# Row scores of the first attention layer's first two heads, taken from the whole K and a masked query instead of the stacks

## The reference

```python
q = proj(query, w_q, b_q)            # (2, 16, 256, 8), query = layernorm(x)
k = proj(key, w_k, b_k)              # (2, 16, 512, 8), key = value = ctx_1024
v = proj(value, w_v, b_v)
scores = einsum('bhqd,bhkd->bhqk', q, k) / sqrt(8)
scores = where(mask == 0, -1e9, scores)
attn = softmax(scores, axis=-1)
x = einsum('bhqk,bhkd->bhqd', attn, v)
```

## Time and profile before

| | us |
|---|---|
| median of 3 runs | 253.52 (252.95 to 254.31) |
| the profiled execution | 252.5 |
| its span, first to last instruction | 250.7 |

### The profile page before, as it was taken

How to read it: one execution, slowest core, us unless ns; L and a number is a source line. 1 busy time by engine, 2 the same in 40 slices (tenths; PEclk the granted TensorE clock), 3 DMA queues, 4 the chain that set the end, 5 groups by cost and what they waited for, 6 DMA issues and landing times.

```text
span 250.7 us, 5109 instructions
## 1 busy us (share of the span) xinstructions
PE 222.7 (89%) x1656; PEld 138.6 (55%) x1656; DVE 185.8 (74%) x578; ACT 156.1 (62%) x228; POOL 79.5 (32%) x228
## 2 busy tenths in 40 slices
PE   2879889999999999989897889999988989989970
PEld 1464445555555558976785444444534447768760
DVE  7779776777777476678558988888775657789974
ACT  6775897677875761521323567877767674796660
POOL 4581445465612100100201252444412042344321
PEclk9999999999999999999999999999999999999999
DMA  6779899921010048600050773300000000000000
GB/s 210 271 220 162 198 164 173 327 67 43 24 65 0 3 90 167 124 0 0 9 165 18 276 230 95 97 3 0 4 0 3 0 1 3 1 0 3 0 21 22
DMA packets 18180, 20.41 MB, mean 81 GB/s; under 512 B 1553, under 2 KB 15609, under 8 KB 17825
## 3 DMA queue, kind: packets, MB, share of 16 engines
q1 hardware_dynamic: 17578, 19.16, 29.7%
q10 hardware_dynamic: 576, 0.94, 1.2%
HBM read 15.90 MB, written 4.19 MB: 80 GB/s over the span
## 4 chain that ended last, share of the span: by engine, by line
PE 53%; DVE 18%; issue 11%; ACT 6%; POOL 5%; DMA 4%; SPq 1%; DVEq 0%; POOLq 0%; ACTq 0%
PE bank L384 10%; PE bank L459 9%; PE bank L437 8%; PE bank L433 5%; PE bank L577 3%; PE bank L557 3%; DVE row_max L885 3%; PE bank L558 3%; DVE st L1071 2%; ACT probs L1396 2%; POOL rs L1719 2%; PE bank L390 2%; PE bank L632 2%; ACT k_stack L1363 2%; DMA aw<-in_attn_w 2%
## 5 line engine op out<-in xcount | busy, mean ns | idle before, releaser
L1396 ACT ACTIVATE probs<-bank 128x1024 f32<-128x1024 f32 x64 | 64.4, 1023 | 16.2 <-PE bank L437 11.1
L882 DVE CUSTOM_DVE_ANT_0 discard<-bank,bias_q 128x512 bf16<-128x512 f32 x64 | 42.5, 689 | 15.8 <-PE bank L384 14.4
L384 PE MATMUL bank<-k_stack,q_stack 72*128 72x512 bf16 x128 | 47.3, 383 | 3.9 <-DVE row_max L885 1.8
L885 DVE TENSOR_REDUCE row_max<-bank 128x1 f32<-128x512 f32 x64 | 42.0, 687 | 9.2 <-PE bank L384 6.7
L437 PE MATMUL bank<-q_stack,k_stack 102*128 102x256 bf16 x256 | 43.7, 272 | 0.2 <-ACT q_stack L1381 0.2
L459 PE MATMUL bank<-probs,v_ext 128*32 128x256 f32 x512 | 37.4, 388 | 0.6 <-ACT probs L1396 0.2
L437 PEld LDWEIGHTS bank<-q_stack,k_stack 102*128 102x128 bf16 x256 | 24.8, 98 | 17.2 <-issue 1.4
L1381 ACT COPY q_stack<-bank 6x512 bf16<-6x512 bf16 x32 | 18.5, 577 | 21.5 <-PE bank L406 21.4
L1637 POOL CAST max_part<-row_max 128x4 bf16<-128x4 f32 x32 | 6.2, 194 | 76.0 <-DVE row_max L885 44.5
L384 PEld LDWEIGHTS bank<-k_stack,q_stack 72*128 72x128 bf16 x128 | 12.2, 96 | 23.4 <-DVE row_max L885 9.8
L433 PE MATMUL bank<-bias_k,idb 128*128 128x512 bf16 x64 | 24.3, 380 | 0.5 <-ACT probs L1396 0.3
(11 more groups left out here) (191 smaller groups left out, 362.9 us busy)
## 6 DMA issues: line engine op xcount, KB each, us to landing
k_stack<-k_bounce SPq DMA_DIRECT2D x9, 384.0 KB
q_bounce<-q_part SPq DMA_DIRECT2D x12, 192.0 KB, 2.6
k_bounce<-early SPq DMA_DIRECT2D x4, 384.0 KB, 2.8
experts_w<-in_wu SPq DMA_DIRECT2D x1, 1024.0 KB, 4.9
early<-in_wu SPq DMA_DIRECT2D x1, 1024.0 KB, 7.2
experts_w<-in_wg SPq DMA_DIRECT2D x1, 816.0 KB, 14.5
experts_w<-in_wu SPq DMA_DIRECT2D x1, 816.0 KB, 16.0
experts_w<-in_wd SPq DMA_DIRECT2D x1, 768.0 KB, 16.6
```

The source lines that it names most:

```text
L384: mm(bank[:, qt, :], q_stack[0:STACK, b, h, qt * 128:(qt + 1) * 128], k_stack[0:STACK, b, h, :], start=True, stop=True).then_inc(for_max, 1)
L882: ins = dve.tensor_tensor_reduce(discard[:, qt, :], bank[:, qt, :], bias_q[:, qt, :], 1.0, LOWEST, ALU.add, ALU.max, o)
L885: ins = dve.tensor_reduce(o, bank[:, qt, :], AX.X, ALU.max)
L1396: act.activation(probs[:, n % (2 * HG), :], bank[:, at:at + 2, :].rearrange("p a n -> p (a n)"), ACT.Exp, scale=SCALE).then_inc(exp_done, 1)
```

## The change

Heads 0 and 1 of layer 1 no longer take their row scores from the stacks. `k_whole` is K as f32 (the sum of its first part and the rest), `q_own[n]` is the f32 query times a column that is one on the partitions of head `n` and zero elsewhere. The product of the two over all 128 partitions is the scores of head `n`. Both are made by POOL in `own_heads`; `head_of`, the columns, is a sum over parts of the identity on DVE. The four products (`own_rows`) are f32 and stand ahead of the loop, and so now do the transposes of the first pair's maxima, head 2's row scores and head 0's column scores. All `keep_busy` calls of layer 1 are gone. On DVE `bias_q` moves ahead of `xT_copy`, `bias_k` comes ahead of the maxima instead of in step 2, and `q_split(0, 1)` moves behind the maxima of head 1. On ACT the first half of the signs moves ahead of `k_evacuate(1)`; the second half goes to POOL (`last_k_sign`), and `q_zero(1)` goes behind POOL's first `max_split`. The projections `v_projection(2)` and `(3)` exchange banks, and the latter's copy moves to step 3.

```diff
+        q_own = [o_sb[:, n, :] for n in range(MG)]
+        k_whole = k_full[0]
+        head_of = sb("head_of", [128, MG])
...
             def score_rows(n, qt):
-                if n == 0 and qt == 0:
+                if n == MG and qt == 0:
                     pe.wait_ge(first_stacked, 16 * (PARTS + len(Q_ROWS)))
-                    pe.wait_ge(k_evacuated, 2)
...
+            def own_rows(n, qt):
+
+                if n == 0 and qt == 0:
+                    pe.wait_ge(own_ready, 1 + MG)
+                    pe.wait_ge(k_evacuated, 2)
+                if n >= 1:
+                    pe.wait_ge(max_done, 2 * (n - 1) + qt + 1)
+                mm(bank[:, qt, :], q_own[n][:, qt * 128:(qt + 1) * 128], k_whole[:, :], start=True, stop=True)\
+                    .then_inc(for_max, 1)
...
-                    rows = l * BEGUN <= s < HEADS
+                    rows = BEGUN <= s < HEADS
+                    opened = l == 0 and s == BEGUN
                     if rows:
                         score_rows(n, 0)
-                    if l == 0 and s < FIRST_LAGS[0]:
-                        keep_busy(5, 2)
-                    if transposes and at_once:
+                    if transposes and at_once and not opened:
                         max_transpose(l * HEADS // MG + (s - 3) // MG)
                         score_rows(n, 1)
-                        keep_busy(5, 2 if s == FIRST_LAGS[0] else 0)
-                    if columns:
+                    if columns and not opened:
                         score_cols(m, range(0, KT // 2))
                         score_cols(m, range(KT // 2, KT))
-                    if rows and not (transposes and at_once):
+                    if rows and (opened or not (transposes and at_once)):
                         score_rows(n, 1)
...
+            v_projection(1, 5)
             transpose_tokens("a0", 1)
-            v_projection(1, 5)
+            own_rows(0, 0)
+            own_rows(0, 1)
             q_projection(0, 1)
-            v_projection(2, OUT)
-            v_projection(3, 3)
-            pe.wait_ge(consts_ready, 1)
-            pe.wait_ge(v_copied[1], 1)
-            keep_busy(5, 5)
+            own_rows(1, 0)
+            own_rows(1, 1)
+            v_projection(2, 3)
+            max_transpose(0)
+            score_rows(2, 0)
+            v_projection(3, OUT)
+            score_cols(0, range(0, KT // 2))
+            score_cols(0, range(KT // 2, KT))
+            score_rows(2, 1)
...
             first_k_rest()
+            heads = idf[:, :].rearrange("p (d h) -> p h d", h=H)
+            dve.tensor_reduce(head_of[:, :], heads[:, 0:MG, :], AX.X, ALU.add).then_inc(head_known, 1)
             first_q_split()
-            normalise("a0", 1, x_sb[:, 1])
-            xT_copy("a0", 1)
-            dve.wait_ge(ld["mask_q"], 16)
-            ts(bias_q[:, :, :], mask_q[:, :, :], 0.0, MASKED, ALU.is_equal, ALU.mult).then_inc(mask_ready, 1)
-            q_split(0, 1)
...
+            normalise("a0", 1, x_sb[:, 1])
+            dve.wait_ge(ld["mask_q"], 16)
+            ts(bias_q[:, :, :], mask_q[:, :, :], 0.0, MASKED, ALU.is_equal, ALU.mult).then_inc(mask_ready, 1)
+            xT_copy("a0", 1)
+            column_bias()
+            head_max(0, 0)
+            head_max(0, 1)
+            head_max(1, 0)
+            head_max(1, 1)
+            dve.wait_ge(q_added, 1)
+            q_split(0, 1)
+            head_max(2, 0)
+            head_max(2, 1)
...
+            k_second_part(0)
             k_sign(0, 0)
-            k_sign(0, 1)
+            k_evacuate(1)
+            v_copy(0, 4)
+            k_evacuate(2)
+            k_evacuate(3)
+            v_copy(1, 5)
+            v_copy(2, 3)
...
+            def own_heads():
+
+                pool.wait_ge(k_rest_ready[0], 1)
+                pool.tensor_tensor(k_whole[:, :], k_part[0][:, 0, :], k_rest[0][:, :], ALU.add).then_inc(own_ready, 1)
+                pool.wait_ge(head_known, 1)
+                pool.wait_ge(rest_kept, 1)
+                pool.tensor_tensor(attT[0][0][:, :], q_part[0][:, 0, :], q_rest[:, :], ALU.add).then_inc(q_added, 1)
+                pool.wait_ge(q_added, 1)
+                for n in range(MG):
+                    pool.tensor_scalar(q_own[n][:, :], attT[0][0][:, :], head_of[:, n:n + 1], None, ALU.mult).then_inc(own_ready, 1)
...
+            own_heads()
             pool.wait_ge(q_parts[0], 1)
             k_split(1, 0)
             k_split(1, 1)
             k_split(1, 2)
-            pool.wait_ge(k_parts[1], 1)
-            q_zero(1)
+            last_k_sign()
             maxima(range(0, HEADS // MG), [
+                (0, lambda: second_query_pads()),
```

More of the change, by code:

```diff
@@ L276, in attention_ffn_kernel @@
         q_early = sem("q_early")
+        head_known = sem("head_known")
+        rest_kept = sem("rest_kept")
+        q_added = sem("q_added")
+        own_ready = sem("own_ready")
         tr1_ready = sem("tr1_ready")
@@ L418, in score_cols @@
                         pe.wait_ge(mask_ready, 2)
-                        pe.wait_ge(v_copied[3], 1)
+                        pe.wait_ge(v_copied[2], 1)
                     if n == 1:
@@ L450, in values @@
                     if g == 0:
-                        pe.wait_ge(v_copied[2], 1)
+                        pe.wait_ge(v_copied[3], 1)
                     if g >= 1:
@@ L1137, in attention @@
                         divide(l * B * NG + group_of(s - 1, OUT_TURN_STEP[l]))
-                    if l * BEGUN <= s < HEADS:
+                    if BEGUN <= s < HEADS:
                         head_max(n, 0)
@@ L1168, in first_q_split @@
                 dve.sem_inc(misc_free, 1)
+                dve.sem_inc(rest_kept, 1)
                 first_k_third()
@@ L1199, in column_bias @@
                 ts(bias_k[:, :, :], mask_k[:, :, :], 0.0, MASKED, ALU.is_equal, ALU.mult).then_inc(mask_ready, 1)
+            normalise("a0", 1, x_sb[:, 1])
[11 more added lines that the diff above has]
+            head_max(2, 1)
             attention(0, [
-                (2, lambda: column_bias()),
                 (27.5, lambda: attT_copy(0, 0)),
@@ L1349, in _ @@
             act.dma_start(row[:, :, :], rows.to_broadcast([128, len(ROW_NAMES), D])).then_inc(ld["row"], 16)
-            k_second_part(0)
-            k_evacuate(1)
-            v_copy(0, 4)
-            k_evacuate(2)
-            k_evacuate(3)
-            v_copy(1, 5)
-            v_copy(2, OUT)
-            v_copy(3, 3)
             def k_sign(b, half):
@@ L1425, in attention @@
                         max_copy(l * HEADS // MG + (s - 3) // MG)
+                    if l == 0 and s == BEGUN:
+                        v_copy(3, OUT)
                     if s in head_of_step[l]:
@@ L1676, in maxima, with last_k_sign, second_query_pads @@
                             f()
+            def own_heads():
[7 more added lines that the diff above has]
+                    pool.tensor_scalar(q_own[n][:, :], attT[0][0][:, :], head_of[:, n:n + 1], None, ALU.mult).then_inc(own_ready, 1)
+            def last_k_sign():
+                n = H // 2
+                pool.wait_ge(k_parts[1], 1)
+                pool.wait_ge(own_ready, 1 + MG)
+                pair = signs[MAX_ROW:ROWS_K, :, :].rearrange("p j c -> p (j c)").bitcast(F32)
+                pool.tensor_copy(k_stack[MAX_ROW:ROWS_K, 0, n:H].rearrange("p (g j) s -> p g (j s)", j=MG).bitcast(F32)
+                                 .rearrange("p g (j s) -> p g j s", j=MG),
+                                 pair.unsqueeze(1).unsqueeze(3).to_broadcast([ROWS_K - MAX_ROW, n // MG, MG, S2 // 2]))\
+                    .then_inc(k_signed[0], 1)
+                pool.wait_ge(k_signed[0], 2)
+            def second_query_pads():
+                pool.wait_ge(max_parts, 1)
+                q_zero(1)
+            own_heads()
             pool.wait_ge(q_parts[0], 1)
```

2 lines of the change are left out of this document (removed).

## The result

| | before | changed |
|---|---|---|
| median, us | 253.56 (20 runs) | 254.93 (20 runs) |
| lowest and highest | 252.89, 257.12 | 253.07, 256.94 |
| ratio | | 1.0054, 95% interval 1.0031 to 1.0076 |
| profiled execution | 252.5 | 253.12 |
| its span | 250.7 | 251.3 |

The change makes the kernel slower by 1.4 us. The forecast was 254.7, +1.2 us. The two profiled executions differ by 0.6 us only. The profile is of the lowest level.

A forecast was written before the change was run, and what follows sets the result against it. The second pair's row-maxima transposes were taken to set the pace, PE being full from 37.8 us. Profiled run 252.5, +1.2 for later transposes, +1.0 from profiled run to median: 254.7 us, range 253.0 to 256.0.

The forecast's parts named there:

- marker: Start of PE's transposes of heads 2 and 3's row maxima, taken as the pace: 28.7 against 27.52, 1.2 us later.
- N: End of DVE's second normalising instruction, forecast at 14.9 against 13.79 before, 1.1 us later.
- S: Start of head 0's first row maximum on DVE, forecast at 17.7 against 19.32 before, 1.6 us won.
- sign of being wrong: The forecast called itself wrong if head 0's first row maximum started before 16.5 us.
- they take turns: DVE and POOL at the start: one holds something shared to its instruction's end while the other waits, delaying N 1.1 us.
- M: End of the four row maxima of heads 0 and 1 on DVE, forecast at S+3.38 = 21.1.
- POOL's sign copy is hidden: POOL's copy of the signs, four times 0.61 from 17.7 to 20.2, ends ahead of M and costs only beyond 21.1.
- T: Start of head 0's column scores on PE, forecast at M+2.45 = 23.55 against 24.14 before.
- rival D: PE's clock at half speed at the start without L390's filler, columns and v_projection +2.7, time 257.4; chance 0.05.
- A: Rival, slower: the query pads' memset precedes q_split(0,1)'s cast, +0.5, another +0.7 with 0.72 masks; 255.2 to 255.9; chance 0.24.
- B: Rival: DVE and POOL turns fall well, two-input instructions not waiting (+0.3) or no waiting (-0.7); 252.8 to 253.8; chance 0.22.
- C: Rival, faster: the exponentials' start sets the pace, head 0's columns 0.6 earlier; 251 to 252.9; chance 0.05.

The follow-up runs named there:

- experiment 5: Two single executions of the changed kernel as it is, to see where PE's clock falls: 254.85 and 253.08 us.
- Experiment 8: Changed kernel with Experiment 4's product order, filler in the second attention and the signs' second half back on ACT: median 251.81 us, ratio 0.9942.
- Experiment 4: Changed kernel with head 2's second row score ahead of v_projection(3) and head 3's first ahead of head 0's columns: lowest 251.80 us, ratio 0.9996.
- experiment 6: Filler products added at the second attention's start: changed kernel 253.56 us, ratio 1.0020; control, the kernel before with the same filler, 253.67 us, ratio 1.0035.
- experiment 1: Changed kernel with keep-warm products put back at the start, where its PE now waits: median 254.73 us, ratio 1.0049.
- experiment 2: Kernel before without layer 1's keep-warm products, which also removed a pair in the second attention: 256.56 us, ratio 1.0129.

## Why the prediction was right, point by point

**What bounds the start: right.** The wait for the stacks is gone, the marker's shift is the shift of the profiled executions (+0.60 and +0.6), and behind the marker the time to the end is the same 223.2 us.

**DVE and POOL block each other: the mechanism right, the price too high.** Forecast N = 14.9 and S = 17.7, measured 14.27 and 16.71; 0.37 of these measured times is the late first projection of Q, which the forecast did not have. In the profile of experiment 5 with the marker at 27.81, S is 16.40, inside what the forecast called a sign of being wrong (before 16.5). POOL's query sum took 1.17 us, not 0.72, because it waited for DVE's third part of K (11.46 to 12.15); that is a DVE instruction with two SBUF inputs, itself not stretched (0.69). The cast behind it stretched to 0.76 and ended 0.15 behind POOL's sum, and the next two-input one took 0.56 (0.43 in the earlier trace rows) beside POOL's first mask. So the row missing before is there now, by POOL's 1.17. It agrees with the Trainium skill (SBUF — State Buffer, Who interferes with whom), by which a DVE instruction with two SBUF inputs contends with a GpSimd one that reads SBUF. The two masks, 2.33 together in the row at 12.78, took 0.94 and 1.40, both above the upper bound of 0.72; how long one takes with DVE idle no row shows. What failed is "they take turns": POOL's second mask was due at 13.71, but the second normalising (to 14.27) and then bias_q (to 14.87) both went first, and the mask ended 0.24 behind bias_q. DVE lost 0.2 us there at most: the two normalising instructions took 0.81 (0.60 alone), bias_q 0.68 (bias_k alone 0.69). That is 1.0 us of S (1.4 if the late start is taken off): the forecast's k_split ahead of the second normalising did not happen. The mechanism itself shows again in bias_k, which ended 0.54 behind POOL's L1673 (16.24), as bias_q did behind L1652 in the earlier trace rows.

**The row maxima: right.** S to M took 3.46 us, 3.38 forecast.

**From M to the columns: 2.71 instead of 2.45.** The step that failed here is "POOL's sign copy is hidden". It took 1.89 us, less than the 2.4 assumed, but began at 18.55 because POOL's k_split was late, and the first split began at 20.50, 0.33 after the maxima and right behind it (before, 0.14 after them). Experiment 8 took it away and got 0.33 back.

**From the columns to the marker: right.** T+5.15 forecast, T+5.24 measured. Experiment 4 shows the mechanism itself.

**The sum: a hit by luck.** The forecast was 252.5 + 1.2 + 1.0. Its step of +1.2 at the marker was mis-sized by the turns: +0.60 in the profiled execution, +0.23 from the first projection of Q on. (Where the K projections are slow the order may cost more: from the same projection to the marker it is 19.13 us in experiment 6's control and 19.73 in experiment 1, though these two differ in filler as well.) Its 1.0 between the profiled execution and the median, taken over from the kernel before, became 1.8. So 252.5 + 0.6 + 1.8 = 254.9: one term was half of what was forecast, and the other nearly twice, by a cause that the forecast gave 0.05, rival D, PE's clock. Not where D put it: the removal of L390 at the start is followed by no fall before 140 us in the four profiles of the changed kernel, while in the kernel before the removal of the same filler costs 3 us (experiment 2). In the changed kernel a fall was seen at 144 to 152 us, in experiment 4 at 141 to 152; where the kernel before loses its clock no profile shows. Above 254.6 us stand 14 of 20, 3 of 10 and 1 of 2 executions of the changed kernel, and 2 of 20, 4 of 26 and 7 of 35 of the kernel before (two of the last disturbed; 254.80 and 255.41 have mean clocks of 0.993 and 0.997 and are no falls).

How much of the 0.54% is the order and how much the falls is an estimate. Executions without a fall, on the chip of experiments 1 to 4, have medians of 253.50 (7 of the changed kernel) and 253.24 (22 of the kernel before): +0.26 us, which fits the 0.23 of the profiles and makes 0.1%. With late filler in both kernels the medians are 253.56 and 253.67, no difference. So roughly 0.1 to 0.2% is the order at the start and the rest the falls. Why they are more frequent is open; the forecast and "The change" had overlooked the two filler products that the diff takes out of the second attention.

**Rivals.** A, the cast against the memset: the cast ran at 21.23 in 0.29, ahead of the memset at 21.65, because the late split had delayed the memset too. B gave the numbers of the profiled execution (S = 16.8 and +0.3 forecast, 16.71 and +0.60 measured, time 253.1 in its 252.8 to 253.8), but not for its reason: two-input instructions do wait. C is refuted: head 0's columns were 1.26 earlier and exponentials with them, and the end was later.

## What to carry to other kernels

When a wait in front of a pipeline is removed, follow one full period behind it: here three 0.2 us products that had stood ahead of a block of columns were pushed behind it, and that cost more than the 1.26 us by which the columns had come earlier. Work moved to POOL has to be added up together with DVE's, not beside it, where their rows show that one waits for the other (here DVE's casts, normalising, masks' biases and two-input sums). And where executions form levels, compare level with level and look at the granted clock by stretch, or a cause in one stage is credited to an edit in another. A line in a loop that both layers share is an edit in both: list by the traces what an edit took out, not by the intention.

## What the runs showed of the hardware that was not expected

- A POOL instruction can wait through two DVE instructions in a row: L1714's second, due at 13.71, ended at 15.11 behind bias_q's 14.87. Waiting first did not mean being next, and the two masks took 2.33 or 2.34 us in all eight profiles that have them.
- PE's granted clock fell to near 0.5 for some microseconds between 141 and 152 us, after stretches at 0.91 and 1.00 (first rows of the fences of experiments 4 and 5); it came in some executions of a kernel and not in others, and cost 2.0 us in the one of experiment 5 and 3.0 in that of experiment 4, from the marker to the end.
- The first projections' speed varies from execution to execution while the granted clock reads 1.00: three f32 products of 512 columns took 2.74 us in one and 4.37 in another. In experiment 6's profile, where they took 3.77, the clock reads 0.66.
